# Recurrent attention and gated feed-forward layer: the output projections of one batch are moved from beats 4 to 7 to beats 7 to 10 of the next

## The chip, the cores and the metric

The kernel runs on 1 core of one Trainium2 chip. The metric is the device time of a run in microseconds (us), median over runs. TensorE (PE in the profile, PEld for its weight loads) multiplies matrices; VectorE (DVE), ScalarE (ACT) and GpSimd (POOL) work elementwise; SyncE (SP) issues all transfers here, in one order.

## The reference

For each of 4 batches of 512 tokens with 512 features, in float32:

```python
xn = layernorm(x)
q, k, v = heads(xn @ w_qkv)                  # 16 heads of 32
q, k = rope(rmsnorm(q) * q_gamma), rope(rmsnorm(k) * k_gamma)
s = softmax(mask(q @ k.T / sqrt(32))) @ v @ w_out      # causal
gate = silu(xn @ W(wq_gate, s_gate).T)       # W(q, s) = (q - 128) * s[:, None]
up = xn @ W(wq_up, s_up).T                   # 1408 hidden features
g = silu((gate * up) @ W(wq_down, s_down).T)
out = x + s * g
```

## The kernel before, in words

Every engine has one program, written out in order, and engines wait for each other at counting semaphores. After a fill (`fill`), 65 **beats** follow, `beat(0, c)` for c = 0 to 64. A beat carries the attention of one head, unit j = c: 16 units make a batch (4 groups of 4 heads). In beat c PE does, in this order: scores of unit c in three parts (`scores_t`, L1346), products of its exponentials with v (`p_v`, L1361) for units c-1 and c, score maxima of unit c+4 (`maxima`, L1382 on PE, L1061 on DVE), the transposes of q and k of unit c+5 (`turn`, L1333) and the q, k, v projection of unit c+7 (`project`, L1321). Matmuls are split into high and low parts in fp32r, so most operands come in pairs (`on_h`, `on_l`; `xnt_h`, `xnt_l`): ACT writes the high part, DVE the low part by a subtraction.

Three more kinds of work are laid into the beats by tables:
- **Gate halves** (`gate_half`, L1424): one half is 8 matmuls of 512 columns for a 128-wide slice of the gate or up projection, into the bank `GU_PS`. A batch has 22. `FIRST` says in which beat they begin (5 beats before the batch), `PER_BEAT` how many a beat takes. `gate` (ACT), `gated` (DVE) read the bank.
- **Output projections** (`out_proj`, L1400): 4 a batch, 12 matmuls of 512 columns each in three parts, into the bank `W_PS`, which the transposes of q and k use as well. For batch b they stand in beats 16b+20 to 16b+23 (`at(c, 20)`), beats 4 to 7 of the next batch. `s_evac` (L783) empties the bank, `s_store` writes it to DRAM. The last batch's stand in the tail.
- **Transposes of normalised x** (`xn_turn`, L1290): four tiles of the next batch, two each in beats 9 and 10 of a batch (`xt_at`), the even tile into `W_PS`, the odd one into `GU_PS`. ACT copies the high part (L716), DVE makes the low part (`xt_low`, L1001), and PE may write the bank again after the semaphore `xt_lo` has counted it.

The first batch's gate weights are integers. SyncE loads one (`int_load`, L332), ACT turns it into fp32r (`gu_weights`, L804), and `first_batch` stores it to DRAM for the later batches (L337) and loads the one three further on. In SyncE's order the transfers of the softmax denominators stand between: `den_out`, `den_in` (L398), and `den_back` (L408), which spreads 4 rows of `rd_dram` over the 128 partitions of `rdb`. `gather` (L386, L387) collects a head's output, POOL sums it (`out_sum`, L635) and multiplies by `rdb` (`norm`, L640), ACT and DVE split it (`o_high` L771, `o_low` L1073).

From beat 57 the down projection (`down`, L1449 and L1450) begins for the first batch; the tail after beat 64 does the rest, with `scaled` (L1236) freeing its banks and `high` (L825), `low` (L1100) splitting hidden features that come back from DRAM.

Of the kernel before, what the change touches and what calls it, by code (L numbers as in the profile page):

```python
# [21 lines left out]
G = 4  # L22
# [31 lines left out]
PER_BEAT = ((2,) * 11,) + ((1, 2, 2, 2, 2, 2, 2, 2, 2, 1, 1, 1, 1, 1),) * 3  # L54
# [20 lines left out]
def build(nc, x, w_qkv, w_out, q_gamma, k_gamma, w_gu, s_gate, s_up, w_down, s_down,  # L75
          cos_tab, sin_tab, ident, mask_w, s_dram, rd_dram, wg_dram, hf_dram, out):
    top = ExitStack()
    with top:
# [70 lines left out]
        sdb = sb("sdb", [P, H])  # L149
# [88 lines left out]
        SPLIT_HF = {54: (0,), 55: (1,), 56: (2,), 59: (3,), 60: (4,), 61: (5,), 63: (6, 7)}  # L238
# [85 lines left out]
        def _(sp):  # L324
# [104 lines left out]
            def beat(r, c):  # L429
# [7 lines left out]
                first_batch(half_at(c, 0))  # L437
                first_batch(half_at(c, 1))
# [260 lines left out]
        def _(act):  # L699
# [78 lines left out]
            def s_evac(b, t, bank=W_PS):  # L778
# [190 lines left out]
        def _(dve):  # L969
# [133 lines left out]
            def beat(r, c):  # L1103
# [573 lines left out]
```

## Time and profile before

| what | value |
|---|---|
| median of 3 runs | 693.9 us (689.15 to 695.75) |
| profiled execution | 696.0 us, its span 694.3 us |
| mean granted TensorE clock | 0.985 |
| ScalarE busy | 456.5 us (66%) |
| GpSimd busy | 412.4 us (59%) |
| HBM read, written | 59.09 MB, 25.82 MB |

Busy shares are averages over the fill (46.4 us), the beats (to about 604 us) and the tail. In a row of the timeline the bracket at the end gives how long the engine was idle before it, and what it waited for. The granted clock is 1.00 at 2.4 GHz and 0.50 at 1.2 GHz.

### The profile page before, as it was taken

The page shows a single profiled execution, that of the slowest core. Times are in us where ns is not written, and L with a number is a line of the kernel's source. Part 1 is how long each engine was busy: PE and PEld are TensorE (multiplying, and loading weights), DVE is VectorE, ACT ScalarE, POOL GpSimd, SP SyncE. Part 2 cuts the span into 40 slices and gives each one's busy share as a digit, 9 for nine tenths or more (in the row PEclk, how much of TensorE's full clock was granted, in tenths as well). Part 3 has the DMA queues.
Part 4 walks back from the last instruction along what each step waited for, and adds up shares of the span by engine and source line. Part 5 has one row for each costly group of instructions (what it writes and reads, how often), then busy time and mean ns, then how long its engine had stood idle before and what let it go on. Part 6 is the DMA issues. An engine that isn't in the chain of part 4 may idle for free.

```text
span 694.3 us, 12569 instructions
## 1 busy us (share of the span) xinstructions
PE 660.8 (95%) x3690; PEld 557.0 (80%) x3690; DVE 543.0 (78%) x1345; ACT 456.5 (66%) x1013; POOL 412.4 (59%) x591
## 2 busy tenths in 40 slices
PE   8889997989999999899999998999999988989997
PEld 6778885878888888788888887888888866767886
DVE  6796885898788879997879789978796796545856
ACT  3587884787676667876766668777667676632541
POOL 7967684777665667876666658766665583500000
PEclk9999998999999999999999999999999999999999
DMA  8545434414434332244332332244453514458895
GB/s 277 200 141 203 150 109 144 153 32 139 122 108 123 82 103 77 62 139 122 99 112 83 94 97 52 57 124 146 132 151 94 171 58 122 121 157 278 291 314 198
DMA packets 62531, 94.40 MB, mean 136 GB/s; under 512 B 12032, under 2 KB 24320, under 8 KB 62336
## 3 DMA queue, kind: packets, MB, share of 16 engines
q1 hardware_dynamic: 62464, 93.59, 43.7%
q8 instruction: 31, 0.51, 0.3%
q14 instruction: 36, 0.29, 0.1%
HBM read 59.09 MB, written 25.82 MB: 122 GB/s over the span
## 4 chain that ended last, share of the span: by engine, by line
PE 72%; POOL 8%; DMA 6%; DVE 5%; issue 4%; ACT 3%; SPq 1%; POOLq 0%; DVEq 0%; ACTq 0%
PE bank L1424 22%; PE bank L1321 14%; PE bank L1361 8%; PE bank L1400 7%; PE bank L1382 5%; PE bank L1450 4%; PE bank L1449 4%; PE bank L1346 4%; PE bank L1333 4%; POOL rr L607 3%; POOL pp L627 2%; DMA rdb<-rd_dram 1%; DMA hf_raw<-hf_dram 1%; DVE pp L1039 1%; DVE bank L1061 1%
## 5 line engine op out<-in xcount | busy, mean ns | idle before, releaser
L627 POOL TENSOR_SCALAR_AFFINE_SELECT pp<-pp 128x256 fp32r<-128x256 f32 x256 | 110.1, 442 | 152.0 <-DVE pp L1039 151.7
L1061 DVE CUSTOM_DVE_ANT_0 bank<-bank,msk_w 128x128 f32<-128x128 f32 (+3 forms) x256 | 121.0, 508 | 41.3 <-PE bank L1382 40.8
L1039 DVE TENSOR_TENSOR pp<-pf,pp 128x512 fp32r<-128x512 f32 (+1 forms) x192 | 134.9, 703 | 9.6 <-ACT pp L758 9.5
L757 ACT ACTIVATE pf<-bank 128x512 f32<-128x512 f32 (+1 forms) x192 | 100.6, 524 | 35.4 <-PE bank L1346 32.6
L1321 PE MATMUL bank<-wq,xnt_h 128*128 128x384 f32 x512 | 112.3, 341 | 9.3 <-DVE qn L1019 7.0
L607 POOL TENSOR_TENSOR rr<-ss,half 128x8 f32<-128x8 f32 x64 | 108.1, 1690 | 18.2 <-DVE ss L1007 18.0
L758 ACT ACTIVATE pp<-bank 128x512 fp32r<-128x512 f32 (+1 forms) x192 | 101.0, 526 | 0.0
L1361 PE MATMUL bank<-pp,va 128*65 128x512 f32 (+3 forms) x512 | 98.8, 312 | 2.0 <-POOL pp L627 1.9
L1424 PE MATMUL bank<-xnt_h,wgu 128*128 128x512 f32 x352 | 99.9, 406 | 0.6 <-DVE g L1089 0.5
L1321 PEld LDWEIGHTS bank<-wq,xnt_h 128*128 128x128 f32 x512 | 88.4, 188 | 14.0 <-issue 10.1
L1424 PE MATMUL bank<-xnt_l,wgu 128*128 128x512 f32 x352 | 98.0, 401 | 0.0
L1424 PEld LDWEIGHTS bank<-xnt_l,wgu 128*128 128x128 f32 x352 | 67.4, 192 | 16.6
L1449 PE MATMUL bank<-wd,ht_h 128*128 128x512 f32 (+1 forms) x187 | 71.6, 388 | 2.5 <-DVE yt L1236 2.5
L1361 PEld LDWEIGHTS bank<-pp,va 128*65 128x65 f32 x512 | 58.6, 137 | 18.5 <-POOL pp L627 3.2
L1450 PE MATMUL bank<-wd,ht_l 128*128 128x512 f32 (+1 forms) x187 | 71.8, 389 | 0.0
L1382 PE MATMUL bank<-kst,qst 96*128 96x128 f32 (+3 forms) x256 | 70.5, 347 | 1.3 <-DVE mx L1061 1.1
L1424 PEld LDWEIGHTS bank<-xnt_h,wgu 128*128 128x128 f32 x352 | 62.2, 191 | 10.8 <-issue 0.9
L1321 PE MATMUL bank<-wq,xnt_l 128*128 128x384 f32 x256 | 69.2, 352 | 0.0
L616 POOL TENSOR_TENSOR rb<-qn,sg 128x128 f32<-128x128 f32 x128 | 68.9, 558 | 0.0
L1333 PEld LDWEIGHTS bank<-idr,tt 128*96 128x96 f32 x512 | 49.0, 126 | 21.3 <-issue 11.0
L1346 PE MATMUL bank<-qst,kst 97*128 97x512 f32 (+3 forms) x256 | 61.7, 318 | 1.1 <-DMA qst<-mrow 0.5
L748 ACT ACTIVATE kst<-bank 96x512 fp32r<-96x512 f32 x64 | 38.0, 594 | 37.0 <-PE bank L1333 36.4
(83 smaller groups left out, 1192.5 us busy)
## 6 DMA issues: line engine op xcount, KB each, us to landing
wgu<-wg_dram SPq DMA_DIRECT2D x66, 256.0 KB, 3.1
hf_dram<-g SPq DMA_DIRECT2D x44, 256.0 KB, 3.2
hf_raw<-hf_dram SPq DMA_DIRECT2D x16, 512.0 KB, 7.5
wg_dram<-wgu SPq DMA_DIRECT2D x22, 256.0 KB, 3.3
xr<-x SPq DMA_DIRECT2D x16, 256.0 KB, 4.3
oh<-oraw SPq DMA_DIRECT2D x64, 64.0 KB, 2.0
ol<-oraw SPq DMA_DIRECT2D x64, 64.0 KB, 2.0
rdb<-rd_dram SPq DMA_DIRECT2D x16, 256.0 KB
```

The lines of the kernel that those rows point to most:

```text
L607: pool.tensor_tensor(rr[:, s, :], ss[:, s, :], half[:], ALU.pow).then_inc(rr_ok, 1)
L627: op = pool.affine_select(pp[:, :, a:a + P], pp[:, :, a:a + P], [[0, 2], [1, P]], ALU.is_ge, 0.0, base=0, channel_multiplier=-1)
L757: act.activation(pf[:, tile], bank[:, 0:w], ACT.Exp, scale=SCALE)
L758: act.activation(ph[:, tile], bank[:, 0:w], ACT.Exp, scale=SCALE).then_inc(p_ok, 1)
L1039: dve.tensor_tensor(pl[:, tile], pf[:, tile], ph[:, tile].bitcast(F32), ALU.subtract).then_inc(pl_ok, 1)
L1061: op = dve.tensor_tensor_reduce(bank[:, a * w:(a + 1) * w], bank[:, a * w:(a + 1) * w], msk_w[:, N - w:N], 1.0, -3.0e38, ALU.add, ALU.max, ...
L1321: op = pe.matmul(qkv_bank(n)[:, 0:3 * GC], x_[:, k, t * P:(t + 1) * P], wq[:, g, w_, k, :], start=(a == 0), stop=(a == len(todo) - 1))
L1361: op = pe.matmul(PV_PS[0:VW, j * P:N], va[:, v, j, h, :], part[:, a:a + w], start=(j == 0 and part is ph), stop=(j == 2 and part is pl))
L1382: op = pe.matmul(bank[:, a * w:(a + 1) * w], qst[0:KS, par, h, qb * P:(qb + 1) * P], kst[0:KS, par, h, 0:w], start=True, stop=True)
L1424: op = pe.matmul(GU_PS[:], wgu[:, s, k, :], x_[:, k, :], start=(a == 0), stop=(a == len(todo) - 1))
L1449: pe.matmul(down_bank(t, part)[:, out_], ht_h[s][:, m, cols], wd[:, m, out_], start=(m == 0), stop=False)
L1450: op = pe.matmul(down_bank(t, part)[:, out_], ht_l[s][:, m, cols], wd[:, m, out_], start=False, stop=(m == MT - 1))
```

## The change

1. Gate halves: batches 1 to 3 take two in beats 4 and 5 and one in beat 6 (before: one in each of beats 4 to 8). Output projections stand in beats 7 to 10 (`at(c, 23)`), and in `GU_PS` in place of `W_PS`. Inside a beat their first two parts come after the gate half and the maxima, and in beats 9 and 10 the first waits for `xt_lo` of the odd tile, which has used the same bank.
2. `on4` is a second place for the first head group of even batches.
3. SyncE handles the stores and loads of the gate weights one beat sooner in its order; integers are staged in `sdb`, and `s_down` is loaded in beat 60 instead of the fill.
4. In the fill, PE's second gate half and DVE's weight split `w_low(1, 2)` stand sooner.
5. Around the end of the beats: `scaled(0, 0)` in beat 62; ACT's and DVE's splits of hidden features in another order; the last denominators are sent before the last gather, and the last `rdb` comes in four transfers of 32 partitions.

```diff
-PER_BEAT = ((2,) * 11,) + ((1, 2, 2, 2, 2, 2, 2, 2, 2, 1, 1, 1, 1, 1),) * 3
+PER_BEAT = ((2,) * 11,) + ((1, 2, 2, 2, 2, 2, 2, 2, 2, 2, 2, 1),) * 3
...
-        SPLIT_HF = {54: (0,), 55: (1,), 56: (2,), 59: (3,), 60: (4,), 61: (5,), 63: (6, 7)}
+        SPLIT_HF = {54: (0,), 55: (1,), 56: (2,), 59: (3,), 60: (4,), 61: (5,), 63: (6,)}
+        LOW_HF = {55: (0,), 57: (1,), 58: (2,), 59: (3,), 60: (4,), 61: (5,), 63: (6,)}
...
+        def on_at(i, g):
+
+            return (on4[:, 0, :], on4[:, 1, :]) if g == 0 and i // G % 2 == 0 else (on_h[:, g, :], on_l[:, g, :])
+
+        def out_at(c):
+
+            d, t = at(c, 23)
+            return (d, t) if t is not None and 0 <= d < B - 1 else None
+
         def int_at(q):
 
-            return (s_sb[:, 0, :], s_sb[:, 1, :], spare[:, 0:N])[q % 3]
+            return (s_sb[:, 0, :], sdb[:], spare[:, 0:N])[q % 3]
...
-                sp.dma_start(rdb[:], rd_dram.rearrange("o (h n) -> (o h) n", h=HG).rearrange(
-                    "h (o n) -> h o n", o=1).to_broadcast([HG, HD, N])).then_inc(rb_in, 16)
+                if i < LAST:
+                    sp.dma_start(rdb[:], rd_dram.rearrange("o (h n) -> (o h) n", h=HG).rearrange(
+                        "h (o n) -> h o n", o=1).to_broadcast([HG, HD, N])).then_inc(rb_in, 16)
+                else:
+                    for h in range(HG):
+                        sp.dma_start(rdb[HD * h:HD * h + HD, :], rd_dram[0:1, h * N:(h + 1) * N].to_broadcast([HD, N])
+                                     ).then_inc(rb_in, 16)
...
-                first_batch(half_at(c, 0))
-                first_batch(half_at(c, 1))
...
                     i, h = 4 * r + (c - 1) // 4, (c - 1) % 4
+                    if i == LAST and h == HG - 1:
+                        sp.wait_ge(o_ev, NB)
+                        den_out(i)
                     gather(i, h)
-                    if h == HG - 1:
+                    if h == HG - 1 and i < LAST:
                         den_out(i)
+                first_batch(half_at(c + 1, 0))
                 if k == 1 and there((c - 5) // 4, B * G):
                     den_in((c - 5) // 4)
                 next_load(half_at(c, 0))
                 hidden_store(half_at(c, 0))
+                first_batch(half_at(c + 1, 1))
                 if k == 1 and there((c - 5) // 4, B * G):
                     den_back((c - 5) // 4)
...
+                if c == NB:
+                    o_out()
                 if k == 0 and (c - 8) // 4 % 4 != G - 1 and there(4 * r + (c - 8) // 4, B * G):
                     o_high(4 * r + (c - 8) // 4, (c - 8) // 4 % 4)
-                o_out()
+                if c < NB:
+                    o_out()
...
+            high(7)
+            high(8)
             outer(0, 0)
-            high(8)
             outer(0, 1)
...
+                if c == 62:
+                    dve.wait_ge(sd_in, 16)
+                    scaled(0, 0)
...
-                w_low(1, 2)
                 t_low(1, 1)
...
+                def out_part(part):
+
+                    if out_at(c):
+                        b, t = out_at(c)
                         if part == 0:
-                            w_free()
-                            wait(pe, tk_ev, min(j + 5, NB) if isinstance(j, int) else j + 5)
-                        out_proj(r + d_o, t_o, part)
+                            if t == 0:
+                                pe.wait_ge(hf_ok, MT * (b + 2))
+                            wait(pe, s_ev, 4 * b + t)
+                            for nb, nt in xts[1:]:
+                                pe.wait_ge(xt_lo, 4 * nb + nt + 1)
+                        out_proj(b, t, part)
...
                 gate_half(half_at(c, 0))
+                if xts:
+                    banks(SM_B)
+                out_part(0)
+                out_part(1)
                 banks(SM_T)
-                if t_o is not None or xts:
+                turn_q()
+                if not xts:
                     banks(SM_B)
...
+                if attend:
+                    scores_t(r, c, 2)
+                out_part(2)
+                if proj:
+                    project(r, c + 7, 0)
...
                 turn(0, 0, 1)
+                gate_half(1)
                 project(0, 4, 1)
                 maxima(0, 0, (0,))
                 turn(0, 1, 0)
-                gate_half(1)
                 turn(0, 1, 1)
```

The changed order at three places. PE, beat 25 (and, with other sizes, 26, 41 and 42), before, from the second maxima of the beat to the projection of unit c+7 (`L1382` maxima, `L1333` transposes of q, `L1346` scores):

```order
L1382 MATMUL bank<-kst,qst 128x256 [waits sm_ok]
L1382 MATMUL bank<-kst,qst 128x256
L1333 MATMUL bank<-idr,tt 96x128 [waits tk_ev,tl_ok,xt_lo]
L1333 MATMUL bank<-idr,tt 96x128 x3
L1346 MATMUL bank<-qst,kst 128x256 [waits p_ok]
L1321 MATMUL bank<-wq,xnt_h 128x384 [waits vh_ok,vl_ok,sq_ok,qn_ok,xt_lo,xt_hi]
L1321 MATMUL bank<-wq,xnt_h 128x384 x3
```

and now (line numbers of the changed kernel; `L1407` maxima, `L1425` output projection):

```order
L1407 MATMUL bank<-kst,qst 128x256 [waits sm_ok]
L1407 MATMUL bank<-kst,qst 128x256
L1425 MATMUL bank<-wo_h,on 128x512 [waits xt_lo,s_ev]
L1425 MATMUL bank<-wo_h,on_h 128x512 x3
L1425 MATMUL bank<-wo_l,on 128x512
L1425 MATMUL bank<-wo_l,on_h 128x512 x3
L1358 MATMUL bank<-idr,tt 96x128 [waits tk_ev,tl_ok,xt_lo]
L1358 MATMUL bank<-idr,tt 96x128 x3
L1371 MATMUL bank<-qst,kst 128x256 [waits p_ok]
L1425 MATMUL bank<-wo_h,on 128x512
L1425 MATMUL bank<-wo_h,on_l 128x512 x3
L1346 MATMUL bank<-wq,xnt_h 128x384 [waits vh_ok,vl_ok,sq_ok,qn_ok,xt_lo,xt_hi]
```

Between the maxima and the transposes of q now stand 8 matmuls of the output projection, and the first of them waits for `xt_lo`, that is for DVE's low part of the odd tile; 4 more stand after the scores.

SyncE, end of beat 5 and beginning of beat 6 (`wg_dram` store of a weight tile, `w_gu` load of an integer tile), before:

```order
L386 DMA oh<-oraw 32x512 [waits os_ok,o_ev]
L387 DMA ol<-oraw 32x512
L398 DMA rd_dram<-rd 128x16 [waits rd_ok]
L408 DMA rdb<-rd_dram 128x1x512 [waits w_lp,rd_out]
L337 DMA wg_dram<-wgu 128x512 [waits wgc_ok]
L332 DMA s_sb<-w_gu 128x512 [waits wgc_ok]
L337 DMA wg_dram<-wgu 128x512 [waits wgc_ok]
L332 DMA spare<-w_gu 128x512 [waits wgc_ok]
```

and now:

```order
L398 DMA oh<-oraw 32x512 [waits os_ok,o_ev]
L399 DMA ol<-oraw 32x512
L349 DMA wg_dram<-wgu 128x512 [waits wgc_ok]
L344 DMA sdb<-w_gu 128x512 [waits wgc_ok]
L410 DMA rd_dram<-rd 128x16 [waits rd_ok]
L349 DMA wg_dram<-wgu 128x512 [waits wgc_ok]
L344 DMA spare<-w_gu 128x512 [waits wgc_ok]
L421 DMA rdb<-rd_dram 128x1x512 [waits w_lp,rd_out]
```

Both pairs of store and load now stand ahead of the `rdb` transfer; the first stands right behind the gather.

ACT, from beat 63 on, before:

```order
L757 ACTIVATE pf<-bank 128x256 [waits pv_ok,st_full]
L758 ACTIVATE pp<-bank 128x256
L825 ACTIVATE ht_h<-hf_raw 128x1024 [waits hf_in0,st_full]
L825 ACTIVATE ht_h<-hf_raw 128x1024 [waits hf_in1]
L771 ACTIVATE on_h<-on 128x512 [waits on_ok]
L766 ACTIVATE oraw<-bank 65x512 [waits pv_ok]
L831 ACT_TABLE_LOAD
L831 ACTIVATE gt<-yt 128x512 [waits y_ok]
L825 ACTIVATE ht_h<-hf_raw 128x768 [waits hf_in2]
L831 ACTIVATE gt<-yt 128x512 [waits y_ok]
```

and now:

```order
L780 ACTIVATE pf<-bank 128x256 [waits pv_ok,st_full]
L781 ACTIVATE pp<-bank 128x256
L848 ACTIVATE ht_h<-hf_raw 128x1024 [waits hf_in0,st_full]
L789 ACTIVATE oraw<-bank 65x512 [waits pv_ok]
L794 ACTIVATE on_h<-on 128x512 [waits on_ok]
L848 ACTIVATE ht_h<-hf_raw 128x1024 [waits hf_in1]
L848 ACTIVATE ht_h<-hf_raw 128x768 [waits hf_in2]
L854 ACT_TABLE_LOAD
L854 ACTIVATE gt<-yt 128x512 [waits y_ok] x2
L848 ACTIVATE ht_h<-hf_raw 128x1024 [waits hf_in3,pv_ok]
```

The evacuation of the last head (`oraw`) now stands behind one split of hidden features, not two.

## Rows read from the trace of the kernel before

**Rows 1.** Page, part 1: engine, busy us, share of the span, instructions.

```profile
PE 660.8 (95%) x3690; PEld 557.0 (80%) x3690; DVE 543.0 (78%) x1345; ACT 456.5 (66%) x1013; POOL 412.4 (59%) x591
```

**Rows 2.** Busy by stretch: stretch, length, then busy and count per engine, PEclk, DMA.

```profile
101.08:118.07 16.99, 11.78 (x54) 9.28 (x53) 10.38 (x26) 7.05 (x16) 11.15 (x14) 0.80 0.45 156
...
515.09:578.22 63.13, 59.59 (x336) 49.74 (x335) 49.72 (x128) 43.55 (x99) 40.97 (x55) 0.97 0.34 102
...
562.55:571.79 9.24, 7.17 (x33) 5.15 (x32) 9.05 (x24) 6.50 (x16) 8.60 (x12) 0.83 0.10 33
...
609.43:694.30 84.87, 75.58 (x335) 61.91 (x334) 51.52 (x71) 29.73 (x41) 2.54 (x2) 0.96 0.76 251
```

**Rows 3.** Busy by stretch, columns as before: beats 20 to 27, one row each.

```profile
231.22:241.07 9.85, 9.85 (x58) 8.38 (x57) 8.06 (x23) 5.40 (x13) 6.18 (x9) 1.00 0.25 77
241.07:250.74 9.67, 9.67 (x58) 8.35 (x57) 7.49 (x23) 6.73 (x16) 6.04 (x9) 1.00 0.28 88
250.74:260.62 9.88, 9.88 (x57) 8.57 (x56) 6.59 (x18) 6.01 (x15) 5.19 (x9) 1.00 0.36 110
260.62:270.83 10.21, 10.21 (x59) 8.64 (x57) 8.80 (x25) 6.83 (x16) 7.25 (x10) 1.00 0.38 116
270.83:278.35 7.52, 7.18 (x47) 6.20 (x45) 7.28 (x21) 6.26 (x17) 6.24 (x9) 1.00 0.09 21
278.35:285.30 6.95, 6.13 (x46) 5.58 (x45) 6.95 (x21) 6.24 (x16) 5.29 (x9) 1.00 0.24 78
285.30:293.05 7.75, 6.76 (x45) 5.83 (x44) 7.30 (x19) 6.26 (x16) 6.95 (x10) 1.00 0.19 49
293.05:300.51 7.46, 7.46 (x46) 6.41 (x45) 6.58 (x17) 5.87 (x15) 5.70 (x9) 1.00 0.14 41
```

**Rows 4.** The chain of waits, beat 21: start us, us, what it was.

```profile
241.99 0.94 PE bank L1400 x4
...
243.63 1.87 PE bank L1424 x8
```

**Rows 5.** Timelines of PE and DVE, beats 25, 26: start, us, engine, line, operation [idle before].

```profile
280.93 0.41 PE L1333 MATMUL bank<-idr,tt 128*96 128x128 f32 x4
...
282.35 0.94 PE L1321 MATMUL bank<-wq,xnt_h 128*128 128x384 f32 x4 [0.82 <-DVE qn L1019]
...
282.13 0.67 DVE L1001 TENSOR_TENSOR xnt_l<-bank,xnt_h 128x512 fp32r<-128x512 f32 x1
...
288.08 0.48 PE L1333 MATMUL bank<-idr,tt 128*96 128x128 f32 x4
...
289.47 0.68 DVE L1001 TENSOR_TENSOR xnt_l<-bank,xnt_h 128x512 fp32r<-128x512 f32 x1
```

**Rows 6.** Timelines of SyncE's queue, ScalarE and PE, beat 6.

```profile
104.30 0.60 SPq L408 DMA_DIRECT2D rdb<-rd_dram  x1
...
105.46 0.43 SPq L332 DMA_DIRECT2D s_sb<-w_gu  x1
...
112.01 0.63 ACT L804 ACTIVATE wgu<-s_sb 128x512 fp32r<-128x512 int32 x1 [6.39 <-DMA s_sb<-w_gu]
...
113.26 0.64 PE L1333 MATMUL bank<-idr,tt 128*96 128x128 f32 x4 [4.74 <-ACT qst L743]
```

**Rows 7.** Timeline of PE in the fill.

```profile
27.85 0.97 PE L1321 MATMUL bank<-wq,xnt_h 128*128 128x384 f32 x4 [1.58 <-DVE wq L974]
```

**Rows 8.** Busy by stretch, a stretch of the tail at the lower clock.

```profile
613.10:616.40 3.30, 3.30 (x9) 2.55 (x9) 1.41 (x2) 0.67 (x2) 1.20 (x1) 0.50 0.27 65
```

**Rows 9.** Timelines of PE and GpSimd in the tail.

```profile
611.91 0.50 PE L1449 MATMUL bank<-wd,ht_h 128*128 128x512 f32 x1 [2.48 <-DVE yt L1236]
...
626.51 1.88 PE L1400 MATMUL bank<-wo_h,on_h 128*128 128x512 f32 x4 [2.55 <-ACT on_h L771]
...
624.44 1.26 POOL L640 TENSOR_TENSOR on<-on,rdb 128x512 f32<-128x512 f32 x1 [10.14 <-DMA rdb<-rd_dram]
```

**Rows 10.** Page, part 6: out<-in, issue, count, KB each, us to landing.

```profile
oh<-oraw SPq DMA_DIRECT2D x64, 64.0 KB, 2.0
```

More of the change, by code:

```diff
@@ L148, in build @@
         hsc = sb("hsc", [P, 2, MT])
-        sdb = sb("sdb", [P, H])
+        with ExitStack() as under:
+            sdb = tiles(under)("sdb", [P, H])
+        on4 = sb("on4", [P, 2, N], F32R)
         msk_w = sb("msk_w", [P, N], BF16)
@@ L770, in o_high @@
                 act.wait_ge(on_ok, i + 1)
-                act.activation(on_h[:, g, :], on[:], ACT.Copy).then_inc(onh_ok, 1)
+                act.activation(on_at(i, g)[0], on[:], ACT.Copy).then_inc(onh_ok, 1)
             def m_evac(i, par):
@@ L776, in m_evac, with s_evac @@
                 act.activation(mrow[:], W_PS[0:(HG - 1) * TB, 0:P], ACT.Copy, scale=-1.0).then_inc(mt_ok, 1)
-            def s_evac(b, t, bank=W_PS):
+            def s_evac(b, t, bank=GU_PS):
                 n = 4 * b + t
@@ L1094, in wd_weights, with scaled @@
                 dve.tensor_scalar(wd[:, m, :], wd_raw[:, m, :], -ZERO, None, ALU.add).then_inc(wd_ok, 1)
+            def scaled(b, t, part=0):
+                n, cols = 4 * b + t + part, columns(b, t, part)
+                dve.wait_ge(dn_full, n + 1)
+                wait(dve, g_ok, n - 1 - part)
+                dve.tensor_tensor(yt[:, t % 2, cols], down_bank(t, part)[:, cols], sdb[:, cols], ALU.mult).then_inc(y_ok, 1)
             def low(v):
@@ L1191, in fill @@
                 gated(0)
+                w_low(1, 2)
                 unit_rms(2, 0)
@@ L1229, in _ @@
             run_beats(dve, beat)
-            def scaled(b, t, part=0):
-                n, cols = 4 * b + t + part, columns(b, t, part)
-                dve.wait_ge(dn_full, n + 1)
-                wait(dve, g_ok, n - 1 - part)
-                dve.tensor_tensor(yt[:, t % 2, cols], down_bank(t, part)[:, cols], sdb[:, cols], ALU.mult).then_inc(y_ok, 1)
             def finish(b, t, part=0):
@@ L1246, in finish @@
                 dve.tensor_tensor(res[:, s, cols], res[:, s, cols], xs[:, t, 0, cols], ALU.add).then_inc(res_ok, 1)
-            dve.wait_ge(sd_in, 16)
-            scaled(0, 0)
+            low(7)
             scaled(0, 1)
@@ L1285, in xn_turn @@
                     wait(pe, xt_lo, n - 1)
+                    if b > 1:
+                        wait(pe, s_ev, 4 * (b - 2) + 2 + t // 2)
                 else:
@@ L1391, in max_turn, with out_proj @@
                 pe.transpose(W_PS[0:(HG - 1) * TB, 0:P], mx[:, TB:], idf[:]).then_inc(mt_full, 1)
-            def out_proj(b, t, part, bank=W_PS):
+            def out_proj(b, t, part, bank=GU_PS):
                 if t == 0 and part != 1:
                     wait(pe, onl_ok if part else onh_ok, 4 * b + 4)
-                todo = [(o_, w_, g) for o_, w_ in ((on_h, wo_h), (on_h, wo_l), (on_l, wo_h)) for g in range(G)]
+                todo = [(a, w_, g) for a, w_ in ((0, wo_h), (0, wo_l), (1, wo_h)) for g in range(G)]
                 m = len(todo) // 3
                 for a, (o_, w_, g) in list(enumerate(todo))[part * m:part * m + m]:
-                    op = pe.matmul(bank[:], o_[:, g, t * P:(t + 1) * P], w_[:, g, :],
+                    op = pe.matmul(bank[:], on_at(4 * b + g, g)[o_][:, t * P:(t + 1) * P], w_[:, g, :],
                                    start=(a == 0), stop=(a == len(todo) - 1))
@@ L1413, in gate_half @@
                     wait(pe, xt_lo, 4 * b + 4)
+                    if b > 1:
+                        wait(pe, s_ev, 4 * (b - 1))
                 if b == 0:
@@ L1463, in turn_q @@
                         w_free()
-                        if t_o is not None and there(r + d_o, B):
-                            pe.wait_ge(s_ev, 4 * (r + d_o) + t_o + 1)
                         for b, t in xts[:1]:
@@ L1472, in turn_k @@
                         turn(r, c + 5, 1)
[L1474 to L1476 removed]
+                def out_part(part):
+                    if out_at(c):
+                        b, t = out_at(c)
                         if part == 0:
[L1478 to L1480 removed]
+                            if t == 0:
[4 more added lines that the diff above has]
+                        out_proj(b, t, part)
                 def w_free():
```

62 lines of the change are left out of this document (18 added, 44 removed).

## Prediction

> **What bounds the kernel now.** I read the page first: PE is busy for 660.8 of 694.3 us [rows 1]. The change removes no arithmetic, so it can only win back PE's idle time and the time that PE works at the lower of its two clocks. The stretches say where these are [rows 2]: PE idles 5.2 us in beat 6, 3.5 in beats 52 to 58 and 9.3 in the tail. The reader should see the mean clock beside them: 0.80 in beat 6, 0.83 in beat 57, 0.96 in the tail. Then the beats that the move touches, one by one [rows 3]: beats 20 to 23 are solid PE, 9.7 to 10.2 us each, beats 24 to 26 leave it 0.34, 0.82 and 0.99 us of idle, and in beat 25 DVE has none at all (6.95 busy of 6.95).
>
> A fall of the clock costs more than the wait ahead of it. In the tail PE was idle for 2.48 us [rows 9] and a stretch of 3.3 us at 0.50 followed (1.2 GHz) [rows 8], in which half the work was done: 1.7 us lost. Waits of 1.58 [rows 7], 4.74 [rows 6] and 2.55 us [rows 9] were followed by such stretches too, those of 0.82 to 0.99 us in beats 25 and 26 were not [rows 3].
>
> **The move of the output projections.** A gate half (8 matmuls) takes 1.87 us, four matmuls of the output projection 0.94, so 12 take 2.8 [rows 4]. From the rows of beats 20 to 27 [rows 3]:
> - Beats 4 and 5 give 2.8 and get 1.9: 8.9 and 8.7 us.
> - Beat 6 gives 2.8: PE 7.1. DVE gets one more gating operation (0.7) on its 6.59, so DVE and PE are even; with small waits 7.6.
> - Beat 7 gives one half: 8.3, taken as 8.5, since DVE has 8.1 there.
> - Beat 8 gives a half and gets a projection: 7.18 + 0.9 = 8.1, its idle 0.34 filled.
> - Beats 9 and 10 get 2.8 each, and a new wait. PE comes to the place of the projection where it now begins the transposes of q, at 280.93, 2.6 us into the beat [rows 5]. The bank is free when DVE has ended the low part of the odd tile, at 282.80, 4.45 us into the beat. That chain (ACT's copy, DVE's first tile, a maximum, a subtraction, qn, the second tile) starts from PE's own projection in the beat before, so DVE's new slack does not shorten it. The wait is 1.9 us, and behind it on PE stand the transposes, scores and projections of the beat, for which ACT and DVE wait. Beat 9: 6.13 + 2.8 + 1.9 = 10.8. In beat 10 PE arrives at 288.08 and DVE ends at 290.15, 2.1 us later; part of it is DVE waiting behind a POOL sum that a longer beat 9 takes away, so 1.6: 6.76 + 2.8 + 1.6 = 11.2. The old waits for qn (0.82 and 0.95) are gone, being shorter than the new ones.
> - Beat 11 stays at 7.46.
>
> Sum 71.3 against 69.3: **+2.0 a batch**, so +4.0 for the two batches that have both kinds of work. The bounds of the wait are 0.8 (the old idle alone) and 3 us. Then the clock: four new waits of 1.6 to 1.9 us, above the 1.58 that was followed by a fall. I take three falls at 1.7, **+5.1**; the ends are 0 and 13.6 (four falls of twice the length; the one behind 4.74 us lasted some 6.8, as 0.80 over 17 us says [rows 2]).
>
> The Trainium skill, page "TensorE: Matmul & The Clock Gate", section "HAM oscillation", ties the fall to idle gaps longer than any of the four new waits. By it these beats would cost +4.0 and not +9.1. The trace disagrees: falls came behind 1.58 and 2.5 us.
>
> **Beat 6.** SyncE issues the integer load at 105.46, behind the `rdb` transfer of 104.30. It lands for ACT at 112.01 after 6.39 us of waiting, and PE waits 4.74 [rows 6]. The load is now issued two transfers behind the gather, at about 103, and is not behind `rdb`. A gather's 64 KB land in 2.0 us [rows 10]; for 256 KB with little ahead I estimate 3 to 4 us, so it lands at 106 to 107, and ACT wants it at 105.6. Late next would be ACT by about 1 us, of which PE, whose wait was 1.65 us shorter than ACT's, sees nothing. PE's busy 11.78 us hold 4.8 at half clock, 2.4 lost, so beat 6 becomes 9.4 in place of 16.99: **-7.6** (ends -8.5 and 0, if the wait stays).
>
> **Fill.** The wait of 1.58 us for a weight split goes, and the half-clock stretch behind it, since DVE makes the split 3 us sooner: 3.3 at most. But PE then meets the next transposes, whose operand DVE gives no sooner. **-1.5** (0 to -3.3). The earlier gate half fills part of that gap.
>
> **Beats 52 to 58.** The third batch's projections leave full beats for beats 55 to 58, with no transposes of x beside them and so no wait for a bank. There are 3.5 us of idle and, at 0.97 over 63 us, 1.9 us lost to the clock [rows 2]. DVE is busy for 9.05 of 9.24 us in beat 57, so that beat stays: **-3.5** (-1 to -5.4).
>
> **Tail.** Two waits, 2.48 us for `scaled(0, 0)` and 2.55 for `on_h`, each with a fall of the clock: 8.4 us [rows 9]. The first goes: `scaled` is now in beat 62, ahead of DVE's wait for hidden features, and `s_down` has been loaded for two beats. The second hangs on `rdb`, for which POOL waits 10.14 us. POOL got it at 624.44. The last head's evacuation and the denominators now go about 2 us sooner, and each of the four transfers has the size and shape of a gather's, which lands in 2.0 us [rows 10]: issued from 613.9 on at 0.6 us each, behind one load of hidden features, they land by 618. Sum and split bring `on_h` to about 620, when PE, with 4.2 us less of waits and clock ahead of it, comes to the projection. **-7.0** (-3 to -8.4); late next would be the low parts of the next hidden features, by a few tenths.
>
> The Trainium skill, "DMA: Bandwidth & Descriptors", section "Rules for kernel authors", says that an outermost dimension under 16 confines a transfer to as many DMA engines; the old `rdb` transfer has 4 there, the new ones 32. No row here shows the engines one by one; the term would be the same by it.
>
> Costed at nothing: `on4` (no instruction more), the bank `GU_PS` for `s_evac` (same ACT operation, in a later beat), three more `rdb` issues of 0.6 us (SyncE waits anyway there), `s_down` in beat 60.
>
> **Sum.** +4.0 + 5.1 - 7.6 - 1.5 - 3.5 - 7.0 = -10.5. From 696.0 for the profiled execution this is 685.5. That run lies 2.1 us above the median; I take 1.5 of it off, since a share of its waits may be its own: **684 us** against 693.9.
>
> **Rivals.**
> 1. *The clock holds* in beats 25, 26, 41, 42: 684 - 5 = 679 us. For it: 0.95 us did no harm. Against: 1.58 did. Chance 0.20.
> 2. *The load wait of beat 6 stays* (the change does not do what it says): the load is still behind the gather, which waits for POOL's sum until the end of beat 5. 684 + 7.6 = 692. Against: `rdb` is behind it now. Chance 0.10.
> 3. *The tail gives nothing back*, as ACT's wait for the hidden features of beat 63 still holds up the last evacuation: 684 + 7 = 691. Chance 0.10.
> 4. *Slower*: the new bank wait in beats 25, 26, 41, 42 grows to 3 us and PE's clock stays down behind each for as long as in beat 6 (3.4 us lost). That is 4 x 6.4 - 3.5 of old idle + 0.4 in beats 4 to 8 = 22.5, against 19.6 gained elsewhere: 696.0 + 2.9 - 1.5 = 697. It decides from 5.8 us a wait. For it: DVE has no slack in beat 25 now. Against: the two beats before it get lighter for DVE. Chance 0.06.
>
> The forecast itself has 0.54 and its own range 680 to 689.
>
> **Range and chances.** 1% is 6.9 us, about what a measurement of this kernel tells from no change. Faster than 687.0: 0.85 of the forecast (0.46), all of rival 1 (0.20), and 0.02 of rivals 2 and 3: 0.68. The rest within 1%: 0.26. Slower than 700.8: rival 4 where it is at its worst, with what I have not thought of: 0.06. Range 675 to 692: it leaves out rival 4 and a half of rivals 2 and 3.
>
> **What would show it.** PE's first output projection in beats 25, 26, 41 and 42 with an idle of 1.6 to 1.9 us, released by DVE's `xnt_l`, and PEclk 0.50 behind it; beats 20 to 27 at 71 us or more; no ACT wait for `w_gu` above 1 us and beat 6 near 9.4; in the tail no wait for `yt` or `on_h` above 1 us, and `rdb` behind its issue by some 3 us. The prediction is wrong if those four waits are under 1 us (DVE's chain was not fixed to PE), or if another wait of over 1.3 us appears in the fill, where the clock would fall again.

## The result

The changed kernel takes **688.7 us** (median of 20 runs, 687.0 to 692.0), the kernel before 692.1 in its 20 runs of the same session (689.15 to 695.75). The ratio is 0.9955 (95% interval 0.9941 to 0.9969): 3.4 us less, where 9.9 had been forecast. 688.7 lies in the range of 675 to 692; the size of the gain was wrong.

The profiled execution took 688.69 us, span 687.0, clock 0.993. First its page, part 1 (engine, busy us, share of the span, instructions):

```profile
PE 655.4 (95%) x3690; PEld 552.2 (80%) x3690; DVE 543.4 (79%) x1345; ACT 457.4 (67%) x1013; POOL 412.1 (60%) x591
```

PE was busy for 5.4 us less than in [rows 1] with as many matmuls: it worked less at the lower clock. Then the stretches, to be laid beside [rows 2, 3] (stretch, length, then busy and count of PE, PEld, DVE, ACT, POOL, then PEclk, DMA): beats 0 to 5, beat 6, beats 20 to 27, of these 20 to 26 one by one, beat 41, beats 52 to 58, of these beat 55, and the tail from beat 63.

```profile
44.93:100.60 55.67, 54.09 (x311) 45.45 (x309) 42.80 (x123) 44.98 (x103) 40.60 (x58) 1.00 0.49 162
100.61:110.61 10.00, 9.67 (x54) 7.77 (x53) 9.54 (x26) 7.29 (x16) 8.54 (x13) 1.00 0.62 190
223.72:296.18 72.46, 67.16 (x405) 57.74 (x404) 58.88 (x163) 49.98 (x117) 48.49 (x71) 1.00 0.23 68
...
223.72:232.47 8.75, 8.75 (x54) 7.60 (x53) 8.44 (x25) 6.49 (x17) 6.16 (x9) 1.00 0.37 117
232.47:241.29 8.82, 8.82 (x54) 7.57 (x52) 7.36 (x23) 6.29 (x15) 5.85 (x9) 1.00 0.09 32
241.29:249.61 8.32, 7.48 (x45) 6.42 (x44) 6.94 (x18) 4.98 (x11) 5.59 (x9) 1.00 0.48 135
249.61:258.55 8.94, 8.60 (x51) 7.24 (x49) 8.51 (x26) 6.03 (x15) 6.33 (x10) 1.00 0.36 99
258.55:267.04 8.49, 8.04 (x50) 6.94 (x49) 7.60 (x21) 6.42 (x17) 7.47 (x10) 1.00 0.22 73
267.04:277.81 10.77, 8.88 (x57) 7.72 (x56) 6.79 (x20) 6.94 (x17) 6.63 (x11) 1.00 0.07 19
277.81:288.72 10.91, 9.14 (x58) 7.85 (x56) 6.66 (x18) 6.96 (x17) 4.75 (x7) 1.00 0.19 61
...
412.20:424.52 12.32, 10.42 (x57) 8.84 (x56) 6.68 (x20) 6.97 (x17) 6.64 (x11) 0.86 0.07 18
...
515.61:576.88 61.27, 58.41 (x337) 49.58 (x336) 49.10 (x128) 43.36 (x99) 39.52 (x55) 0.97 0.34 102
540.43:553.43 13.00, 10.30 (x51) 8.49 (x49) 7.17 (x20) 6.86 (x16) 6.63 (x10) 0.87 0.52 164
...
597.85:686.98 89.13, 82.34 (x381) 66.39 (x379) 55.14 (x75) 35.03 (x50) 6.91 (x8) 0.98 0.79 261
```

Beat 6 has lost its long wait, beats 25, 26 and 41 are longer as foreseen, and beat 55, 10.2 us before, now takes 13.00 with 2.7 us of idle. Next PE's waits by releaser (us in total, times, longest):

```profile
PE bank L1425 <- DVE xnt_l L1023: 7.4, 4, 1.9
...
PE bank L1404 <- DVE mx L1083: 2.7, 1, 2.7
```

The first row is the new wait for the odd tile, four times. Its timelines in beat 25, PE and DVE (start, us, engine, line, operation [idle before]), answer to [rows 5]:

```profile
271.64 0.47 PE L1425 MATMUL bank<-wo_h,on 128*128 128x512 f32 x1 [1.90 <-DVE xnt_l L1023]
```

```profile
270.48 0.41 DVE L1041 TENSOR_TENSOR qn<-bank,rr 128x256 f32<-128x256 f32 x1
270.82 0.68 DVE L1023 TENSOR_TENSOR xnt_l<-bank,xnt_h 128x512 fp32r<-128x512 f32 x1
```

PE stands 1.90 us until DVE has ended the tile. In beats 26, 41 and 42 it is 1.77, 1.90 and 1.79. The second row of the waits was not foreseen. Its chain, PE, ACT and DVE in beat 55 and SyncE before it:

```profile
546.82 0.27 PE L1404 MATMUL bank<-idf,mx 128*4 128x128 f32 x1 [2.70 <-DVE mx L1083]
```

```profile
543.68 1.06 ACT L848 ACTIVATE ht_h<-hf_raw 128x1024 fp32r<-128x1024 f32 x1 [2.96 <-DMA hf_raw<-hf_dram]
```

```profile
545.39 0.43 DVE L1055 TENSOR_TENSOR tt<-qp,tt 128x256 fp32r<-128x256 f32 x1 [3.96 <-ACT tt L759]
```

```profile
535.14 0.60 SPq L421 DMA_DIRECT2D rdb<-rd_dram  x1
535.78 0.47 SPq L384 DMA_DIRECT2D wd_raw<-w_down  x1
536.37 0.38 SPq L391 DMA_DIRECT2D hf_raw<-hf_dram  x1
```

ACT's first split of hidden features, the last thing of beat 54, waits 2.96 us for its load. DVE waits behind ACT, PE behind DVE. In the kernel before the load was issued at 537.49, 1.1 us later, and ACT met no wait:

```profile
545.03 1.06 ACT L825 ACTIVATE ht_h<-hf_raw 128x1024 fp32r<-128x1024 f32 x1
```

By the landing records it was there at 544.18, 0.85 us before ACT began. Beat 54 took 9.86 us then and takes 7.22 now: the move has taken a projection from it, and with it the time that covered the load. Last, beat 6 (ACT) and the tail (PE, POOL), which answer to [rows 6, 9]:

```profile
105.61 0.63 ACT L827 ACTIVATE wgu<-sdb 128x512 fp32r<-128x512 int32 x1 [0.53 <-DMA sdb<-w_gu]
```

```profile
612.15 0.50 PE L1477 MATMUL bank<-wd,ht_h 128*128 128x512 f32 x1 [0.54 <-DVE ht_l L1129]
...
619.92 0.47 PE L1425 MATMUL bank<-wo_h,on_h 128*128 128x512 f32 x1 [0.97 <-ACT on_h L794]
```

```profile
616.86 2.26 POOL L663 TENSOR_TENSOR on<-on,rdb 128x512 f32<-128x512 f32 x1 [5.58 <-DMA rdb<-rd_dram]
```

ACT's 6.39 us in beat 6 have become 0.53, and PE's longest waits of the tail, 2.48 for `yt` and 2.55 for `on_h`, have become 0.54 (now for `ht_l`) and 0.97.

### The profile page after: what moved, and what is told of

Same layout as the page of the kernel before. It is cut to its first block, busy times and chain, and to the rows that moved or that the text cites. A ratio compares the mean times of both kernels' runs of the same rounds, so it can differ in the third digit from the quotient of the medians.

```text
span 687.0 us, 12581 instructions
## 1 busy us (share of the span) xinstructions
PE 655.4 (95%) x3690; PEld 552.2 (80%) x3690; DVE 543.4 (79%) x1345; ACT 457.4 (67%) x1013; POOL 412.1 (60%) x591
## 4 chain that ended last, share of the span: by engine, by line
PE 57%; DVE 12%; POOL 10%; issue 7%; DMA 7%; ACT 5%; SPq 1%; DVEq 0%; ACTq 0%; POOLq 0%
PE bank L1451 20%; PE bank L1346 13%; PE bank L1386 7%; PE bank L1407 4%; DMA hf_raw<-hf_dram 4%; PE bank L1358 4%; PE bank L1371 4%; PE bank L1425 3%; POOL rr L630 3%; DVE pp L1061 2%; POOL pp L650 2%; POOL rb L639 2%; DVE bank L1083 1%; DVE ht_l L1129 1%; POOL ra L636 1%
## 5 line engine op out<-in xcount | busy, mean ns | idle before, releaser
L1346 PE MATMUL bank<-wq,xnt_h 128*128 128x384 f32 x512 | 112.3, 341 | 2.3 <-DVE qn L1041 1.8
L1451 PE MATMUL bank<-xnt_h,wgu 128*128 128x512 f32 x352 | 98.2, 401 | 2.2 <-DVE g L1107 1.7
L1451 PE MATMUL bank<-xnt_l,wgu 128*128 128x512 f32 x352 | 96.5, 396 | 0.0
L1346 PEld LDWEIGHTS bank<-wq,xnt_h 128*128 128x128 f32 x512 | 89.1, 189 | 5.4 <-issue 3.5
L1407 PE MATMUL bank<-kst,qst 96*128 96x128 f32 (+3 forms) x256 | 70.6, 347 | 1.0 <-DVE mx L1083 0.7
L1477 PE MATMUL bank<-wd,ht_h 128*128 128x512 f32 (+1 forms) x187 | 70.2, 381 | 0.7 <-DVE ht_l L1129 0.7
L1478 PE MATMUL bank<-wd,ht_l 128*128 128x512 f32 (+1 forms) x187 | 70.2, 381 | 0.0
L1346 PE MATMUL bank<-wq,xnt_l 128*128 128x384 f32 x256 | 69.8, 355 | 0.0
L766 ACT ACTIVATE qst<-bank 96x512 fp32r<-96x512 f32 x64 | 37.8, 591 | 39.6 <-PE bank L1358 39.5
```

The lines of the kernel that those rows point to most:

```text
L1346: op = pe.matmul(qkv_bank(n)[:, 0:3 * GC], x_[:, k, t * P:(t + 1) * P], wq[:, g, w_, k, :], start=(a == 0), stop=(a == len(todo) - 1))
L1407: op = pe.matmul(bank[:, a * w:(a + 1) * w], qst[0:KS, par, h, qb * P:(qb + 1) * P], kst[0:KS, par, h, 0:w], start=True, stop=True)
L1451: op = pe.matmul(GU_PS[:], wgu[:, s, k, :], x_[:, k, :], start=(a == 0), stop=(a == len(todo) - 1))
```

## The experiments

Theory A: the move costs what the wait for the odd tile, the wait in beat 55 and the clock behind them make, and the rest of the change gains independently. The rivals are in the expectations. Lengths are in us; a "fall" is a stretch of PE at 0.50. Each kernel was timed beside runs of the kernel before.

**before_again**: the kernel before, unchanged.

> The kernel before, unchanged, for a second profile. Its profiled execution took 696.0 us, 3.9 above its median of 692.1. Theory A: the wait for the integer load in beat 6 (ACT 6.39 us) is there in every execution and what is typical is fewer or shorter stretches at half clock; then beat 6 is 13 to 17 us again and the span is about 690. Theory B: the wait itself differs from run to run (the load lands 2 to 4 us sooner); then beat 6 is under 13 us here, and the change could win only that much by issuing the load sooner.

693.93 us, span 692.2. Beat 6 and the half-clock stretch in it:

```profile
99.40:115.87 16.47, 11.80 (x53) 9.30 (x52) 10.38 (x26) 7.05 (x16) 11.16 (x14) 0.79 0.47 161
109.11:115.94 6.83, 4.87 (x15) 3.73 (x16) 1.99 (x5) 3.29 (x9) 3.51 (x3) 0.50 0.50 189
```

The long wait of beat 6 belongs to the kernel. The fill took 44.7 us and not 46.4 as in the first profile: there the wait of 1.58 us was followed by a fall [rows 7], here the same wait, 1.57 us, was not. Part of what I booked as a gain was this one execution's.

**old_place**: the changed kernel with the output projections and gate halves where they were, and with them the order inside the beats and the bank.

```diff
-PER_BEAT = ((2,) * 11,) + ((1, 2, 2, 2, 2, 2, 2, 2, 2, 2, 2, 1),) * 3
+PER_BEAT = ((2,) * 11,) + ((1, 2, 2, 2, 2, 2, 2, 2, 2, 1, 1, 1, 1, 1),) * 3
...
-            d, t = at(c, 23)
+            d, t = at(c, 20)
...
-            def out_proj(b, t, part, bank=GU_PS):
+            def out_proj(b, t, part, bank=W_PS):
```

> The changed kernel with its output projections, their bank and the gate halves of beats 4 to 8 put back as before; the sooner stores, the fill, the tail and on4 stay. Theory A (the move costs): by the two profiles the move makes beats 20 to 27 3.2 us longer and beats 36 to 43 4.7 longer, and wins 1.9 in beats 52 to 58; without it 688.7 - 6.0 = 683 us. Theory B (the move is neutral and the other parts gave less than their waits were worth): 687 to 690 us.

680.0 us (679.9 to 681.3), ratio 0.9827 (0.9802 to 0.9852). Beats 20 to 27 and 52 to 58:

```profile
222.69:291.88 69.19, 67.00 (x406) 57.93 (x404) 59.03 (x163) 49.59 (x117) 48.76 (x71) 1.00 0.26 76
506.56:569.37 62.81, 59.18 (x336) 49.71 (x335) 49.02 (x128) 43.52 (x99) 38.88 (x55) 0.97 0.36 109
```

The move alone costs 8.7 us (688.7 less 680.0), the other parts alone gain 12, and the time is 3 us under what theory A gave. Beats 0 to 5 take 54.7 as before, against 55.7 now, so that 1.0 is the move's as well; it stands in beats 4 and 5, 0.6 and 0.4 us.

**late_part**: in beats 25, 26, 41 and 42 the whole output projection stands behind the q projection.

```diff
                 if xts:
                     banks(SM_B)
-                out_part(0)
-                out_part(1)
+                else:
+                    out_part(0)
+                    out_part(1)
...
-                out_part(2)
+                if not xts:
+                    out_part(2)
                 if proj:
                     project(r, c + 7, 0)
+                if xts:
+                    for part in range(3):
+                        out_part(part)
```

> The changed kernel; in beats 25, 26, 41 and 42 alone all three parts of the output projection stand behind the transposes of q, the scores and the first half of the projection of unit c+7. Theory A (the wait for xt_lo costs what PE idles): PE waits 0.8 to 1.0 us for qn in place of 1.8 to 1.9 for xt_lo, four times, and no clock falls there: 688.7 - 4.0 - 1.0 = 684 us. Theory B (the beat is set by ACT's and DVE's chain whatever PE does in it): the wait moves to the transposes of k or into the next beat, 688 to 689 us.

681.65 us (681.5 to 683.8), ratio 0.9857 (0.9830 to 0.9884). PE in beat 25, then beats 25 and 26:

```profile
270.97 0.95 PE L1346 MATMUL bank<-wq,xnt_h 128*128 128x384 f32 x4 [0.86 <-DVE qn L1041]
```

```profile
266.97:276.73 9.76, 8.90 (x58) 7.79 (x56) 6.83 (x20) 6.73 (x17) 6.82 (x11) 1.00 0.03 10
276.73:286.58 9.85, 9.12 (x57) 7.96 (x56) 6.67 (x18) 6.85 (x17) 4.76 (x7) 1.00 0.28 81
```

PE meets only the old wait for `qn`: theory A, with 2.4 us more than it gave. 7.0 of the 8.7 us are back, but not all of it from these beats. The two profiled executions are 7.0 us apart too: 4.1 are the four waits, 1.6 the fall that the changed kernel had in beat 41, 0.8 stand in beats 52 to 58, where the wait of beat 55 is still there (2.55 us) but no fall followed, and 0.5 in the tail. So the order of the 12 matmuls is worth 4.1 us of waiting and some falls, 5.7 in this pair of executions.

**high0_late**: the first split of hidden features one beat later.

```diff
-        SPLIT_HF = {54: (0,), 55: (1,), 56: (2,), 59: (3,), 60: (4,), 61: (5,), 63: (6,)}
-        LOW_HF = {55: (0,), 57: (1,), 58: (2,), 59: (3,), 60: (4,), 61: (5,), 63: (6,)}
+        SPLIT_HF = {55: (0, 1), 56: (2,), 59: (3,), 60: (4,), 61: (5,), 63: (6,)}
+        LOW_HF = {56: (0,), 57: (1,), 58: (2,), 59: (3,), 60: (4,), 61: (5,), 63: (6,)}
```

> The changed kernel with ACT's first split of hidden features at the end of beat 55 in place of 54, and DVE's in beat 56 in place of 55. Theory A (in the shorter beat 54 ACT waits 2.96 us for the load, and PE 2.70 behind it, with a fall of the clock): 688.7 - 2.7 - 1.2 = 685 us, no PE idle over 1 us in beat 55. Theory B (the PE wait in beat 55 is DVE's work, not the load): it stays, 688 to 689 us.

686.5 us (685.8 to 688.4), ratio 0.9921 (0.9895 to 0.9947): 2.2 less, where theory A gave 3.9: its mechanism, at little more than half its size. ACT finds its load there, and beats 52 to 58 are 3 us shorter, their clock 1.00 again:

```profile
550.12 1.06 ACT L848 ACTIVATE ht_h<-hf_raw 128x1024 fp32r<-128x1024 f32 x1
```

```profile
516.77:575.02 58.25, 57.03 (x336) 48.21 (x335) 49.50 (x128) 43.28 (x99) 39.59 (x56) 1.00 0.36 107
```

**sp_late**: SyncE handles the first batch's gate weights behind `rdb` again, and in the fill as before.

```diff
+                first_batch(half_at(c, 0))
+                first_batch(half_at(c, 1))
                 next_load(half_at(c - 1, 1))
...
-                first_batch(half_at(c + 1, 0))
...
-                first_batch(half_at(c + 1, 1))
```

> The changed kernel with SyncE's stores and loads of the first batch's gate weights put back a beat, behind rdb, as before; sdb, the move and the tail stay. Theory A (the place in SyncE's order alone made beat 6 short): beat 6 back to 16.5 to 17 us from 10.0, the wait of 4.2 to 4.7 us on PE and the half clock behind it back, total 688.7 + 6.5 = 695.2. Rival B (the third staging place sdb made the load early, the order did not matter): beat 6 stays near 10 and the total 688.7.

697.55 us (696.2 to 699.4), ratio 1.0065 (1.0044 to 1.0085), 7.6 us more than the change by the ratios. ACT, then beat 6:

```profile
111.07 0.63 ACT L825 ACTIVATE wgu<-sdb 128x512 fp32r<-128x512 int32 x1 [5.95 <-DMA sdb<-w_gu]
```

```profile
100.64:117.89 17.25, 11.48 (x53) 9.38 (x52) 9.85 (x26) 7.16 (x16) 11.12 (x14) 0.80 0.46 153
```

Theory A: the order on SyncE made the gain; `sdb` alone, in place of the second half of `s_sb`, does not bring it.

**one_rdb**: the last `rdb` as one transfer.

```diff
-                if i < LAST:
+                if True:
                     sp.dma_start(rdb[:], rd_dram.rearrange("o (h n) -> (o h) n", h=HG).rearrange(
```

> The changed kernel with the last rdb as one transfer of 4 outer rows, as before; the sooner denominators and scaled(0, 0) in beat 62 stay. Theory A (the split makes it land sooner): rdb lands some 3 to 5 us later than now, on_h too, PE waits 3 to 5 us for it ahead of the last output projection in place of 0.97 and the clock falls behind it: 688.7 + 5 = 693. Rival B (the sooner issue did it, the split nothing): 688.7, with the wait under 1.3 us.

692.3 us (691.4 to 695.75), ratio 0.9995 (0.9975 to 1.0015), 2.8 us more than the change. POOL, PE and SyncE in the tail:

```profile
619.89 1.26 POOL L663 TENSOR_TENSOR on<-on,rdb 128x512 f32<-128x512 f32 x1 [9.11 <-DMA rdb<-rd_dram]
```

```profile
621.96 0.71 PE L1425 MATMUL bank<-wo_h,on_h 128*128 128x512 f32 x2 [3.50 <-ACT on_h L794]
```

```profile
612.17 0.59 SPq L421 DMA_DIRECT2D rdb<-rd_dram  x1
```

One transfer is there for POOL 7.7 us after its issue; the four of the changed kernel, issued between 612.83 and 614.6, were all there by 616.86. Theory A in the mechanism, under its size (3.6 us by the medians, 2.8 by the ratios, for some 4 to 5). The tail takes 92.3 us against 89.1: 2.5 more of this wait, and a fall behind it.

**best**: late_part, high0_late, and every `rdb` transfer of the beats in four.

```diff
-                if i < LAST:
+                if False:
                     sp.dma_start(rdb[:], rd_dram.rearrange("o (h n) -> (o h) n", h=HG).rearrange(
...
-                wait(pool, rb_in, 16 * (i + (HG if i == LAST else 1)))
+                wait(pool, rb_in, 16 * HG * (i + 1))
```

> The changed kernel with three edits: in beats 25, 26, 41 and 42 all of the output projection behind the q projection (as in late_part), the first two splits of hidden features both at the end of beat 55 (as in high0_late), and every rdb transfer of the beats as four of 32 partitions, not the last one only. Theory A (the waits are independent and add up): late_part gave -7.0 and high0_late -2.2 against the changed kernel's 688.7, so 679.5, with beats 20 to 27 at 70.4 and beats 52 to 58 at 58 us. Rival B (the wait of beat 55 has another cause when beats 25 to 42 are short, late_part has 60.4 there and no clock fall): only 1 us of high0_late's gain is left, 681. Of the split transfers A says that they change nothing in the beats but that the next load lands a us or two sooner (0 in the total); B says that 48 more issues on SyncE at 0.6 us delay loads and stores and cost 1 to 3 us.

**678.7 us** (678.55 to 680.9), ratio 0.9798 (0.9780 to 0.9816). PE is at full clock from end to end:

```profile
223.97:294.35 70.38, 67.15 (x406) 57.89 (x405) 58.92 (x163) 49.68 (x117) 48.62 (x71) 1.00 0.25 71
510.16:568.50 58.34, 57.18 (x336) 48.23 (x335) 49.51 (x128) 43.24 (x99) 39.65 (x55) 1.00 0.37 108
```

**late_high0**: `best` without the split of the earlier `rdb` transfers.

> best without its split rdb transfers: the late output projection in beats 25, 26, 41, 42 and the first two splits of hidden features both at the end of beat 55. Theory A (the two edits add up, the split transfers give nothing in the beats): 678.7 like best, with beats 20 to 27 at 70.4, beats 52 to 58 at 58.3, no wait over 1 us. Rival B (the split transfers brought the last 2 us): 681, with a wait of over 1 us back in beats 55 to 57.

679.2 us (679.1 to 679.8), ratio 0.9815 (0.9801 to 0.9828): the two edits add up, 9.7 us off the change by the ratios. What the split transfers bring to the time (0.5 us by the medians, 1.2 by the ratios) stays open, since the intervals of the two overlap; in the profiled executions no stretch of the beats is shorter with them.

**old_rdb**: `old_place` with every `rdb` in four.

> old_place (the changed kernel with its output projections left in beats 4 to 7, 680.0 us) with every rdb transfer as four of 32 partitions. If the order on SyncE has slack, 680.0 again, within 0.5. If the single rdb transfer of 4 outer rows is what holds up the loads behind it, beats 52 to 58 (62.8, with a PE wait of 1.6 us in beat 56 and a clock fall) become 61 and the time 678 to 679. If 45 more issues crowd the queue, 682.

679.84 us (679.8 to 680.05), ratio 0.9808 (0.9793 to 0.9822). No gain against 680.0 that can be told from none; beats 52 to 58 take 62.4 (62.8). The wait of 1.61 us and the fall are still there; they stand in beat 57, not in beat 56 as expected here and in old_high0.

**old_high0**: `old_place` with the split of high0_late.

> old_place (output projections left in beats 4 to 7, 680.0 us) with the first two splits of hidden features both at the end of beat 55. Theory A (moving the projections is worth nothing once its waits are gone, 680.0 against best's 678.7): beats 52 to 58 stay 62 to 63, since beats 55 to 58 are filled with gate halves and projections there, 680 within 1 us. Rival B (this edit helps wherever the projections stand): the 1.6 us wait in beat 56 and the clock fall behind it go, 676 to 677, and old_high0 is the best version.

682.4 us (681.3 to 684.7), ratio 0.9863 (0.9843 to 0.9883). Rival B falls, and A's "within 1 us" with it: beats 52 to 58 go from 62.8 to 64.3, beat 56 from 7.97 to 8.90 and beat 57 from 8.51 to 9.27. That the two splits come on top of full beats there is argued, not shown. Where the projections stand in beats 7 to 10 the same edit gains 2.2 us. So the best version with the projections moved takes 678.7 to 679.2 us, and the best with them left 679.8 to 680.0; `best` and old_rdb, timed in one session, differ by 1.1. **The move itself is worth about 1 us, and that with its waits removed.** Even this flatters it: the wait of beat 57 and the fall behind it (1.7 us of clock) are still in the versions that leave the projections, and neither old_rdb nor old_high0, which were to remove them, did so.

## Why the prediction was wrong

Stretch by stretch, us, each cut at the first scores of a beat (each row the lengths of the same stretch in the profiled execution of that kernel):

```
stretch          before  before_again  change  old_place  late_part  late_high0
fill              46.4      44.7        44.9     44.9       44.9       44.7
beats 0 to 5      54.7      54.7        55.7     54.7       55.6       55.7
beat 6            17.0      16.5        10.0      9.9       10.0       10.2
beats 20 to 27    69.3      69.3        72.5     69.2       70.4       70.4
beats 36 to 43    69.2      69.2        73.9     69.2       70.4       70.3
beats 52 to 58    63.1      63.1        61.3     62.8       60.4       58.3
beats 59 to 62    21.6      21.0        21.0     20.9       21.0       21.0
from beat 63      94.4      95.2        89.1     89.2       88.6       88.3
```

The forecast of the profiled executions was -10.5; they differ by 7.3 (694.3 and 687.0).

- **Beat 6**, -7.6 foreseen: -7.0. The mechanism holds (sp_late). The load landed just in time, with 0.53 us of ACT's wait.
- **Fill**, -1.5: -1.5. In size right by luck: before_again had 1.7 us less there by itself, since no fall followed its wait. Against an execution without that fall the change wins nothing in the fill (44.7 and 44.9), though the wait is gone: PE idles elsewhere, as the prediction feared of the next transposes.
- **The move in beats 20 to 27 and 36 to 43**, +4.0 for the beats and +5.1 for the clock: together +7.9 (3.2 and 4.7) for 9.1. That the sum came near is luck, for both terms were wrong: without the clock the beats cost 6.3, the clock 1.6. The wait stood where foreseen, released by what was foreseen, at 1.90 and 1.77 us for 1.9 and 1.6, and DVE ended the odd tile 4.46 us into beat 25, where 4.45 had been read. But the beats in front were dearer: 8.3, 8.9 and 8.5 for 7.6, 8.5 and 8.1; in beat 22 PE waits 0.84 us for DVE's gating, where the prediction had priced "small waits" of two engines that are even at 0.5. And of the four waits one was followed by a fall, where three had been taken; over the four profiled kernels that have these waits it was 6 of 16. So in this execution rival 1 (the clock holds, 679) was nearer for the clock than the forecast, but its time missed the dearer beats and all that follows here.
- **Beats 0 to 5**, costed at nothing: +1.0. The prediction looked at the order of beats 4 and 5 only where projections stand in them. In the first batch none do, yet the beats were written anew. That it is the move's is shown (old_place); which piece of the order does it isn't.
- **Beats 52 to 58**, -3.5: -1.9. **This step failed**: "with no transposes of x beside them and so no wait for a bank". True of the bank, but the prediction asked only what the beats that receive the projections wait for, and not what the beat that gives one away had covered. Beat 54 lost 2.6 us, the load for ACT was issued only 1.1 us sooner and landed 0.5 sooner, and there was a wait of 2.7 and a fall. With it removed (high0_late: -2.2 in the median, -3.0 in these beats) the term would have been -4.9.
- **Tail**, -7.0: -5.3, and -0.65 in beats 59 to 62. Both waits went as said. What was mis-sized is in part their rest, 0.54 and 0.97 us where "a few tenths" had been left; the remainder of the 1.7 stays open. That splitting `rdb` does it, and not the sooner issue alone, is shown (one_rdb).
- **From the execution to the median**, -1.5: the profiled execution of before lies 3.9 us above the median of its 20 runs, and the prediction went by a median of 3. The gain shrinks by 1.8 with the median of before (693.9 to 692.1), and by 1.5 since the changed kernel's profiled execution lies on its own median.

The terms sum up: gain foreseen 9.9, less 3.2 for the terms (tail 1.7, beats 52 to 58 1.6, beats 0 to 5 1.0, beat 6 0.6, and 0.1 elsewhere, less 1.2 in beats 20 to 43 and 0.65 in 59 to 62), less 1.5 and 1.8 for the two medians, makes 3.4. Half of the miss is what the executions differ by on their own. The mechanisms of beat 6, of the tail and of the new bank wait were right; that of beats 52 to 58 lacked a wait, and the sizes of the move's two terms were wrong against each other.

## What to carry to other kernels

When work is moved, price the place that gives it away as well: what loads and what chains on other engines did its time cover, and who comes to them sooner now. If a new wait for a bank stands behind a chain that is fixed to the same beat, put the work that needs the bank behind the work that does not: 12 matmuls moved behind the q projection were worth 5.7 us of the 7.0 here. Take a gain out of a wait only after a second profiled execution has shown it again: the wait of the fill was there the next time, the fall behind it was not.

## What the runs showed of the hardware

**The clock.** How long PE idled did not by itself decide whether its clock fell to 0.50 (1.2 GHz). Over the profiled executions of the four kernels that have the wait for the odd tile (the changed one, high0_late, sp_late, one_rdb): waits of 1.89 to 1.91 us were followed by a fall in 6 of 8 cases, those of 1.77 to 1.79 in none of 8. But the wait of 1.61 us in old_place and in old_rdb was followed by one both times, and so was the one of 1.29 in both executions of before (beat 57; there the 0.83 of [rows 2] comes from, which the prediction did not trace), while 1.57 and 1.60 of before_again were not. First old_high0, with a fall behind 1.30 us; then late_part, where 2.55 us of idle was followed by none:

```profile
557.77 0.41 PE L1360 MATMUL bank<-idr,tt 128*96 128x128 f32 x3 [1.30 <-DVE tt L1057]
```

```profile
560.03:563.45 3.42, 3.42 (x8) 2.66 (x9) 2.81 (x8) 1.14 (x3) 3.42 (x6) 0.50 0.01 2
```

```profile
540.93 0.27 PE L1404 MATMUL bank<-idf,mx 128*4 128x128 f32 x1 [2.55 <-DVE mx L1083]
```

```profile
540.93:544.34 3.41, 3.41 (x22) 2.94 (x22) 3.11 (x8) 2.57 (x6) 1.96 (x4) 1.00 0.00 1
544.34:547.75 3.41, 3.31 (x25) 2.85 (x23) 3.40 (x6) 2.62 (x7) 3.33 (x6) 1.00 0.69 193
```

Waits of 0.97 us and less were followed by none in any. What sets the outcome for waits between 1.3 and 2.7 us was not tried. Whether these falls are why times scatter isn't shown: before spread over 6.6 us and the change over 5.0, late_high0, whose longest wait behind the start is 0.96 us, over 0.7; but old_rdb, with its 1.61 us, spread over 0.3, and `best`, without such a wait and at full clock in all four runs, over 2.3. The Trainium skill, page "TensorE: Matmul & The Clock Gate", section "HAM oscillation", ties falls to longer gaps than any of these; the runs disagree, with falls behind 1.30, 1.61 and 1.90 us.

**The broadcast of `rdb` in one transfer holds up those behind it.** The same two loads behind `rdb`, in late_high0 with `rdb` as one transfer of 256 KB with 4 outer rows, then in `best` as four of 64 KB with 32 (KB each, us from issue to landing):

```profile
hf_raw<-hf_dram SPq DMA_DIRECT2D x1, 512.0 KB, 6.9
wd_raw<-w_down SPq DMA_DIRECT2D x1, 256.0 KB, 5.7
```

```profile
hf_raw<-hf_dram SPq DMA_DIRECT2D x1, 512.0 KB, 4.0
rdb<-rd_dram SPq DMA_DIRECT2D x4, 64.0 KB, 2.0
wd_raw<-w_down SPq DMA_DIRECT2D x1, 256.0 KB, 2.9
```

Three more issues of `rdb` stand ahead of them in `best`. Counted from the first issue of `rdb`, the loads are there after 4.6 and 6.3 us in place of 6.3 and 8.1, about 1.8 us sooner. The size alone does not do it: 11 us later in late_high0 the next pair of 256 and 384 KB, with no `rdb` ahead, took 2.9 and 3.5 us. The packet records of one_rdb, from 614.6 to 616.6 us, have four packets of 2 KB in flight nearly all the time, which by their size are of `rdb`, beside some 11 of 1 KB, the hidden features: it moves only about four packets at a time. Whether the 4 outer rows, the broadcast or both make it so was not tried. The time shows hardly any of it, since after high0_late's edit nobody waits for these loads. Beat 6 with the loads behind `rdb` (sp_late) and the wait of one_rdb fit it.
